# A graph layer's neighbour gather: in every fourth pair the last half tile is fetched row by row by SyncE

## What is computed

```python
ef = relu(edge_attr @ We1 + be1) @ We2 + be2
ef = ef * sigmoid(timestamps[:, None] @ Wt + bt)
combined = concatenate([x[row], ef], axis=1)
msg = relu(combined @ Wn1 + bn1) @ Wn2 + bn2
out = segment_sum(msg, col, num_segments=x.shape[0])
result = layernorm(x + (out + x))
```

## Time and profile before

| | |
|---|---|
| Median of 3 runs | 1075.1 us (1071.12 to 1075.13) |
| The profiled execution, its own time | 1073.66 us |
| Its span, first to last instruction | 1071.8 us |
| POOL busy | 797.7 us (74% of the span) |
| PE busy | 867.7 us (81%) |
| DVE busy | 578.2 us (54%) |
| ACT busy | 569.1 us (53%) |
| Mean granted TensorE clock, share of full speed | 0.934 |
| DMA queues of SP, of POOL: share of 16 engines | 24.4%, 19.0% |

### The profile page before, as it was taken

One profiled execution on the slowest core, in us unless ns is written; L12 is line 12 of the kernel. 1 busy time (PEld: TensorE's weight loads), 2 busy tenths in 40 slices (PEclk: granted clock), 3 DMA queues, 4 the chain that ended last, 5 costly groups with the idle time before them and its releaser, 6 DMA issues.

```text
span 1071.8 us, 14843 instructions
## 1 busy us (share of the span) xinstructions
PE 867.7 (81%) x5031; PEld 634.3 (59%) x5032; DVE 578.2 (54%) x1086; ACT 569.1 (53%) x629; POOL 797.7 (74%) x840
## 2 busy tenths in 40 slices
PE   6899999788788788788787797887787878797874
PEld 6676767466456466565555565665565566565654
DVE  4765664554644554644455464555455455365565
ACT  5576674454464464554455464555455546365542
POOL 7777777777777777777777777777777777777772
PEclk9999998898999999998999898999898999898997
DMA  8955444434444344434435434534434534433311
GB/s 247 301 185 170 139 144 140 146 116 131 155 125 152 125 120 148 142 111 147 136 111 158 133 114 123 168 113 137 154 112 126 166 111 140 154 111 122 111 52 43
DMA packets 70428, 148.38 MB, mean 138 GB/s; under 512 B 17511, under 2 KB 45350, under 8 KB 63686
## 3 DMA queue, kind: packets, MB, share of 16 engines
q1 hardware_dynamic: 41126, 89.26, 24.4%
q0 software_dynamic: 26624, 54.58, 19.0%
q10 hardware_dynamic: 2592, 3.48, 0.9%
HBM read 140.85 MB, written 6.40 MB: 137 GB/s over the span
## 4 chain that ended last, share of the span: by engine, by line
POOL 67%; issue 23%; DMA 4%; PE 2%; DVE 2%; ACT 1%; ACTq 0%; DVEq 0%; POOLq 0%
POOL gathered L470 65%; DMA gathered<-node_table,src_e 3%; POOL h L470 1%; POOL raw_own L470 1%; DVE h L1063 1%; PE psS L742 1%; PE psM L784 1%; ACT x_sb L614 1%; PE psH L797 1%; ACT h L532 0%; DMA raw_e<-in_src 0%; PE psS L735 0%; DVEq L370 0%; POOLq L482 0%; ACTq L624 0%
## 5 line engine op out<-in xcount | busy, mean ns | idle before, releaser
L470 POOL DMA_INDIRECT gathered<-node_table,src_e x800 | 766.2, 958 | 243.8 <-issue 241.4
L601 ACT ACTIVATE h<-psH,be_c 128x1024 f32<-128x1024 f32 x104 | 116.0, 1115 | 364.0 <-PE psH L797 363.9
L742 PE MATMUL psS<-onehot,h 128*128 128x128 f32 x1648 | 237.5, 304 | 85.0 <-ACT h L532 81.5
L742 PEld LDWEIGHTS psS<-onehot,h 128*128 128x128 f32 x1648 | 219.9, 215 | 103.6 <-ACT h L532 54.3
L1063 DVE TENSOR_TENSOR h<-psM,gathered 128x1024 f32<-128x1024 f32 (+1 forms) x104 | 122.8, 1183 | 292.8 <-DMA gathered<-node_table,src_e 163.5
L593 ACT ACTIVATE tw<-ew,bt_c,wt_c 128x1024 f32<-128x1024 f32 x104 | 236.0, 2270 | 18.3 <-DVE efw L1080 16.9
L809 PE MATMUL psE<-h,we 128*128 128x512 f32 x416 | 214.6, 640 | 0.0
L784 PE MATMUL psM<-wn,efw 128*128 128x128 f32 x1664 | 210.9, 282 | 3.9 <-DVE h L1063 3.9
L784 PEld LDWEIGHTS psM<-wn,efw 128*128 128x128 f32 x1664 | 203.7, 200 | 4.8 <-DVE h L1063 4.8
L1080 DVE SCALAR_TENSOR_TENSOR efw<-psE,be_c,tw 128x1024 f32<-128x1024 f32 x104 | 133.3, 1282 | 126.5 <-PE psE L809 122.1
L797 PE MATMUL psH<-eaT,we 64*128 64x512 f32 x416 | 123.2, 670 | 43.0 <-DMA gathered<-node_table,src_e 42.9
(11 more groups left out here) (111 smaller groups left out, 336.9 us busy)
## 6 DMA issues: line engine op xcount, KB each, us to landing
ew<-in_edge_weight SPq DMA_DIRECT2D x52, 1024.0 KB
ea<-in_edge_attr SPq DMA_DIRECT2D x52, 512.0 KB
gathered<-node_table,src_e POOLq DMA_INDIRECT x800, 2.5
x_sb<-in_x SPq DMA_DIRECT2D x6, 512.0 KB, 9.6
out_y<-x_sb ACTq DMA_DIRECT2D x12, 256.0 KB
node_table<-gathered SPq DMA_DIRECT2D x7, 256.0 KB
node_table<-h SPq DMA_DIRECT2D x4, 256.0 KB, 4.0
h<-in_x,raw_e POOLq DMA_INDIRECT x16, 6.3
```

What stands on the lines that cost most here:

```text
L470: pool.indirect_dma_start(to, None, rows, bass.IndirectOffsetOnAxis(index, 0)).then_inc(landed, 16)
L601: nc.scalar.activation(h1[:, s % 2, :], psH[:, :, :].rearrange("p r e -> p (r e)"), ACT.Relu, bias=be1_c[:, :]).then_inc(h1_ready, 1)
L742: return nc.tensor.matmul(to, h[:, (k - SUM_LAG) % BODY * PAIR + q, t * C:(t + 1) * C], hot, start=(t == 0), stop=(t == TILES - 1))
```

## The change

For the pairs 8, 12, 16, ... 100 (24 of them; those that `by_rows` names) the eighth gather covers 64 partitions instead of 128. The 64 rows of the upper partitions are fetched by SyncE, each with a DMA of its own of one row, straight into the same place of `gathered`. For this SyncE reads the row number of every edge from `src_rows` into a register, 8 numbers with one load instruction, and each DMA takes its source address from a register. 32 rows (a half) are fetched in an even super, before which SyncE waits for `pre_ready` of pair p-4, and 32 in the odd one after it, both after that super's loads of `ea` and `ew`. VectorE waits in these pairs for the semaphore `rows_in` too.

```diff
+ROW_LOAD, ROWS_BY = 8, P // 2
+ROW_TILE = PAIR * TILES - 1
...
+        def by_rows(p):
+
+            return p % BODY == 0 and p >= SLOTS and p < PAIRS - 1
...
+            def fetch_rows(p, half):
+
+                g, t = p * PAIR + ROW_TILE // TILES, ROW_TILE % TILES
+                j = ORDER[t]
+                if half == 0:
+                    sp.wait_ge(pre_ready, p - (BODY - 1))
+                rows = (P - ROWS_BY) // 2
+                for at in range(ROWS_BY + half * rows, ROWS_BY + (half + 1) * rows, ROW_LOAD):
+                    nodes = nc.values_load_multi_w_load_instructions(
+                        src_rows[g % P:g % P + 1, g // P, at * TILES + j:(at + ROW_LOAD - 1) * TILES + j + 1:TILES],
+                        engines=(mybir.EngineType.SP,), min_val=0, max_val=N - 1,
+                        skip_runtime_bounds_check_because="an edge's source, which the inputs bound")[1]
+                    for r, node in enumerate(nodes):
+                        sp.dma_start(gathered[at + r:at + r + 1, g % SLOTS, t * C:(t + 1) * C],
+                                     table[bass.ds(node, 1), :]).then_inc(rows_in, 16)
+
+            sp.wait_ge(src_in, 48)
+            wait_table(sp)
             for m in range(2, SUPERS):
                 sp.wait_ge(eaT_ps, (m - 1) * 2)
                 load_edges(m % 2, (m - 1) * SE)
                 sp.wait_ge(tw_ready, (m - 1) * 2)
                 load_weights_of(m % 2, (m - 1) * SE)
+                p = m // 2 * BODY
+                if by_rows(p):
+                    fetch_rows(p, m % 2)
...
-                        gather_rows(gathered[:, p % BODY * PAIR + q, t * C:(t + 1) * C], table,
-                                    src_e[:, p * PAIR + q, t:t + 1], landed)
+                        rows = ROWS_BY if by_rows(p) and q * TILES + t == ROW_TILE else P
+                        gather_rows(gathered[0:rows, p % BODY * PAIR + q, t * C:(t + 1) * C], table,
+                                    src_e[0:rows, p * PAIR + q, t:t + 1], landed)
...
+                    if place == 0 and not (isinstance(i, int) and i < 2):
+                        dve.wait_ge(rows_in, (i - 1) * (16 * (P - ROWS_BY)))
```

More of the change, by code:

```diff
@@ L197, in gnn_kernel @@
         gather_in = [[sem(f"gather_in{i}_{part}") for part in range(2)] for i in range(BODY)]
+        rows_in = sem("rows_in")
         last_gather_in = [sem(f"last_gather_in{i}") for i in range(1 + TILES)]
```

## The result

The changed kernel takes 1243.47 us (median of 6 runs, 1241.74 to 1246.45) against 1074.61 us (6 runs, 1071.12 to 1078.11): ratio 1.158, 95% interval 1.1561 to 1.1598, 169 us more. The direction was forecast, the size was not: 1243 lies above the range, and 34 us more had been forecast.

The account below looks back on a forecast made before the run. GpSimd was taken to bound the kernel before, SyncE's ring after: 81.4 + 24 turns of 41.0 (984.0) + a tail of 40.6 gave span 1106.0, +34.2 us, so 1109 us on the median; range 1065 to 1195.

Parts of the forecast that it names:

- What bounds the kernel before: GpSimd's gathers, 1.26 us each with pause and 40.4 us a turn of four pairs, never waiting for data or place.
- The half gather: On GpSimd, 24 gathers with half their rows save 0 to 0.47 us each; 5.7 us in all was taken.
- rival 1: SyncE stays hidden and the half gather pays: 1069 us, or 1064 at half price; chance 0.15.
- rival 2: SyncE hidden, but a 64-row gather takes as long as one of 128: 1075 us, no change; chance 0.14.
- The ring: Add of pair p-4, first half, two loads, second half, landing, add of pair p: 41.0 us a turn.
- the point that decides: 39.3 us a turn, the pace of adds before; the ring reaches it at 0.553 us a row, making SyncE the bound.
- the price of a row: SyncE's issue time for one fetched row, register instruction, DMA and share of the register load: 0.58 us.
- the MOVE: Instruction of 0.038 + 0.035 us at line 624's register-address DMAs; left out of the row's price, as the built list had none.
- The register load: On SyncE, eight registers in one load: 0.316 + 7 x 0.20 = 1.72 us, 1.76 with pause.
- The sum: Add of pair 4 at 81.4, 24 turns of 41.0, tail 40.6: span 1106.0 us, 1109 us on the median.
- Rival 3: SyncE's issue is dearer, DMA 0.35 us: 0.68 a row, 1268 us; with a MOVE too, 1380; chance 0.17.
- rival 4: Rows land one after another, 2 us each: a turn over 130 us, the run over 3000; chance 0.04.

Follow-up runs that it names:

- The runs expected at 35.6, 38.9, 41.2 and 45.8 us a turn: Changed kernel with 48 rows, 1072.48 us; register address only for the first DMA behind each load, 1083.64; 56 rows in loads of 7, 1135.08; loads of 16, 1204.8.

## Why the prediction was right and where it failed

**What bounds the kernel before** was right: without SyncE's rows nothing changed but 1 or 2 us.

**The half gather** was put at 0 to 0.47 us each, 5.7 us in all. It is 0.041, 1 us in all: near the lower end. The rule of the Trainium skill that had been set beside it (page DMA: Bandwidth & Descriptors, section Anatomy of one DMA), that many descriptors can be had before their cost shows, holds in this case's trace: 0.8 ns a row beside 0.84 us fixed. So small a saving meant that the change could gain next to nothing even with SyncE hidden, so rival 1 had no 5 us to win; of the two hidden cases only rival 2 was open.

**The ring and the point that decides** were right. The runs expected at 35.6, 38.9, 41.2 and 45.8 us a turn by their sums came out within 1 us a turn of the ring's (39.4 where it is hidden, 39.8, 41.6 and 44.8), though the second of them landed on the slow side of the point and not under it, and the adds stood for SyncE's rows in all 24 pairs.

**The step that failed is the price of a row**, "A row is thus 0.073 + 0.29 = 0.36 us, with its share of the load (1.76 / 8 = 0.22) 0.58 us". It is 21.6 / 32 = 0.67. Two terms of it were mis-sized:
- *"so I leave it out"*, the MOVE. There is one for each of the 1536 DMAs, 0.029 us and on the mean 0.035 of pause, 64 x 0.064 = 4.1 us a turn. Line 624, the only row with addresses from registers, had shown one for each of its 12 DMAs; I trusted a list of the built program, which doesn't print it, over that row. With it in the sum the ring is 41.0 + 4.1 = 45.1.
- *The register load*, 1.76 with pause, is 1.97: eight a turn, 1.7 us. The price of a register was right (0.20, measured 0.204), but the fixed part is 0.30 on SyncE and not the 0.12 that DVE's two rows leave. The Trainium skill, page Runtime: NRT & Kernel Launch, section Instruction fetch mechanics, has about 200 ns a register; the measured slope agrees, but the 1.6 us that the prediction made of it for a load of eight, without a fixed part, is 0.33 under the measured 1.93.

The rest of the turn is small. The DMAs with their pause (0.233 + 0.052 us on the mean; the first behind a load takes 0.27, the others 0.228) and the register instructions cost in all what had been put for them. The loads of `ea` and `ew` add 0.3, and 0.7 goes off because the add comes 1.1 us after the last row's issue and not 1.8. Together 41.0 + 4.1 + 1.7 - 0.4 = 46.4, as measured.

**The sum.** 24 x 5.4 = 130 us of the 138 that the span has over the forecast 1106. The start adds 3 (84.5 instead of 81.4) and the tail 5 (45.7 instead of 40.6 us behind the add of pair 100), where I had taken off 7 us for a quicker end; why only 2 of the 7 came is not shown.

**The rivals.** Rival 3 had the right sign of the error, in its MOVE; its DMA of 0.35 us is refuted (0.23), as is rival 4 by the landing of 1.1 us. That its first form, 0.68 us a row and 1268 us, lies near the measured 0.67 and 1243 is chance: its dearer DMA stands in for the MOVE and the dearer register load. The range ended at 0.63 us a row, and the thinness of the margin was seen as an argument for the faster side alone: the same 5% that made "hidden" likely makes each missed 0.01 us a row worth 15 us on the other side.

## What to carry to other kernels

Count an engine's list, not its busy share: a transfer issued with an address read from memory cost its issuer 0.67 us here, of which 0.25 were the register load and 0.12 address instructions, while the transfer itself could be issued in 0.30. Where two engines hand work to each other once a turn, write the ring out, and find the turn that it must stay under; past it every 0.01 us is multiplied by turns and rows. And before an expensive engine's instruction is made smaller, look at whether its time depends on its size: taking away half the rows of a gather gave back 4% of it.

## What was not expected of the hardware

- An indirect gather's time on GpSimd: 0.85 us for 16 rows, 0.94 for 128, and 0.940 for 72 where 80 take 0.905.
- A register load on SyncE: 0.30 us and 0.204 for each register, the same slope for 7, 8, 14 and 16.
- A one-row DMA with a register address holds SyncE for 0.228 us, one with a fixed address, back to back, for 0.253: the DMA itself is not dearer for its address, the MOVE and the arithmetic ahead of it are.
- TensorE's granted clock over the span fell from 0.934 to 0.861 of full speed, in a run in which it waits 239.4 us (before: 81.5) for ScalarE's `h`, which waits for the late add. The matmuls of line 773 took 338 ns on the mean against 304 before. They are 1% of the chain that ended last and all of TensorE is 4%, so little of the 169 us can lie there; no run separates it.
